# Four projections of two linear-attention layers: fp32 factors split into two rounded parts

## What is computed

```python
xn = layer_norm(x) * norm_w + norm_b
q = xn @ Wq + bq                      # [2, 2048, 512]
k = xn @ Wk + bk + mask               # masked rows far down
v = (xn @ Wv + bv) * mask
q = softmax(q, over one head's columns)
k = softmax(k, over the 2048 rows)
y = q @ (k.T @ v)                     # by head
h = layer_norm(y) * sb_w + sb_b       # then scale and shift by a condition
out = x + silu(h * (1 + scale) + shift) @ Wo + bo
```

## Time and profile before

| | us |
|---|---|
| median of three runs | 5700.12 (5699.62 to 5701.42) |
| profiled execution | 5699.54 |
| its span in the trace | 5697.7 |
| TensorE busy | 5175.6 (91%) |
| VectorE, ScalarE, GpSimd busy | 4163.2, 3142.4, 3289.4 |
| layers 2 and 3, start to end | 4478 to 5088, 5088 to 5698 |

### The profile page before, as it was taken

How to read it: one execution, slowest core, us unless ns; L and a number is a source line. 1 busy time by engine, 2 the same in 40 slices (tenths; PEclk the granted TensorE clock), 3 DMA queues, 4 the chain that set the end, 5 groups by cost and what they waited for, 6 DMA issues and landing times. The chain is left out here.

```text
span 5697.7 us, 58876 instructions
## 1 busy us (share of the span) xinstructions
PE 5175.6 (91%) x18688; PEld 2441.0 (43%) x18688; DVE 4163.2 (73%) x5558; ACT 3142.4 (55%) x5839; POOL 3289.4 (58%) x2200
## 2 busy tenths in 40 slices
PE   7888989888888969989999999999997899989998
PEld 2333333333333324434444444444443455444545
DVE  6999999999999983247777777777763455545454
ACT  4757566665757533327888888888872131312112
POOL 3879797888879761107898898898892000000000
PEclk9999999999999999988999999999998999999999
DMA  4021221212021205321111111111102302021101
GB/s 170 23 104 38 97 88 52 78 49 97 29 104 43 84 11 191 126 82 35 24 35 35 24 35 35 24 35 35 24 13 107 113 26 70 17 106 35 61 26 52
DMA packets 117511, 346.30 MB, mean 61 GB/s; under 512 B 13041, under 2 KB 14289, under 8 KB 102801
## 3 DMA queue, kind: packets, MB, share of 16 engines
q1 hardware_dynamic: 99280, 294.47, 15.8%
q0 software_dynamic: 9216, 33.56, 1.6%
q10 hardware_dynamic: 8704, 14.50, 0.7%
HBM read 274.29 MB, written 67.67 MB: 60 GB/s over the span
## 5 line engine op out<-in xcount | busy, mean ns | idle before, releaser
L425 POOL TENSOR_TENSOR mamba_hc<-mamba_h,mamba_bc 128x1024 f32<-128x1024 f32 x512 | 1218.2, 2379 | 360.7 <-DVE mamba_h L658 307.0
L805 PE MATMUL mamba_y<-mamba_hc,ident 128*128 128x512 f32 x2048 | 997.3, 610 | 272.1 <-POOL mamba_hc L425 269.8
L1282 POOL TENSOR_TENSOR attn_pair_sum<-attn_pair_sum,attn_prob 128x1024 f32<-128x1024 f32 x512 | 1204.2, 2386 | 56.0 <-ACT attn_prob L1397 56.0
L1441 DVE TENSOR_REDUCE attn_mx<-attn_ps_max 128x1 f32<-128x512 f32 x1536 | 966.9, 684 | 318.6 <-PE attn_ps_max L1305 313.7
L1397 ACT ACTIVATE attn_prob<-attn_ps_s 128x512 f32<-128x512 f32 x2048 | 1051.4, 602 | 78.3 <-PE attn_ps_s L1332 78.3
L528 ACT ACTIVATE mamba_da<-mamba_dt,mamba_a_neg 128x512 f32<-128x512 f32 x1024 | 691.1, 689 | 721.6 <-DVE mamba_h L658 718.0
L658 DVE TENSOR_TENSOR_SCAN mamba_h<-mamba_da,mamba_state,mamba_h 128x512 f32<-128x512 f32 x768 | 939.3, 1264 | 1.9 <-ACT mamba_da L528 1.9
L1332 PE MATMUL attn_ps_s<-attn_q_stack,attn_k_stack 100*128 100x512 f32 x2048 | 885.2, 436 | 5.2 <-ACT attn_prob L1397 5.2
L1305 PE MATMUL attn_ps_max<-attn_k_stack,attn_q_stack 98*128 98x512 f32 x2048 | 834.4, 412 | 33.4 <-ACT attn_own_exp L1406 16.6
L805 PEld LDWEIGHTS mamba_y<-mamba_hc,ident 128*128 128x128 f32 x2048 | 366.3, 191 | 856.0 <-POOL mamba_hc L425 458.2
L648 DVE TENSOR_TENSOR mamba_h<-mamba_du,mamba_bc 128x1024 f32<-128x1024 f32 x512 | 618.6, 1208 | 65.2 <-POOL mamba_state L427 56.8
(11 more groups left out here) (240 smaller groups left out, 6545.7 us busy)
## 6 DMA issues: line engine op xcount, KB each, us to landing
mamba_bc<-bc_dram SPq DMA_DIRECT2D x64, 1024.0 KB, 7.2
mamba_w<-in_in_proj_w_T SPq DMA_DIRECT2D x16, 2048.0 KB, 7.7
qk_parts<-qkv_pair POOLq DMA_DIRECT2D x64, 512.0 KB, 3.2
attn_k_stack<-qk_parts SPq DMA_DIRECT2D x96, 256.0 KB
attn_q_stack<-qk_parts SPq DMA_DIRECT2D x96, 256.0 KB
mamba_x_in<-in_x SPq DMA_DIRECT2D x16, 1024.0 KB, 5.5
mamba_w<-in_out_proj_w_T SPq DMA_DIRECT2D x8, 2048.0 KB, 8.4
lin_norm_x<-x_after_L SPq DMA_DIRECT2D x16, 1024.0 KB, 6.0
```

Of the source, the lines that this page charges most:

```text
L425: nc.gpsimd.tensor_tensor(hc[:, gs % HC_SLOTS, :, :], h[:, gs % H_SLOTS, :, :], bc[:, g, G:2 * G, :], ALU.mult).then_inc(s["hc_done"], 1)
L805: mm = nc.tensor.matmul(y[ct % 2][:, :], ident[:, :], hc[:, gs % HC_SLOTS, j, :], start=(g == 0 and j == 0), stop=(g == NG - 1 and j == G ...
L1282: nc.gpsimd.tensor_tensor(pair_sum[(hd * NGRP + g) % 2][:, at], first[:, at], prob[unit % SLOTS][:, at], ALU.add).then_inc(s["sum_done"], 1)
L1441: nc.vector.tensor_reduce(to, ps_max[seq % BANKS][:, :], AX.X, ALU.max, negate=own_block(i)).then_inc(s["bank_read"], 1)
```

## The change

Each factor of the four projections is kept as two tiles of the rounded type: a first part (`xn_first`, `w_first`), the value rounded, and a second part (`xn_second`, `w_second`), the value less its first part, rounded. A product becomes three: first by first, first by second, second by first. The fourth is left out.

- Weights: ScalarE rounds a loaded weight (`cut_w`), GpSimd subtracts (`split_w`). The raw weights land in parts of `v_all` and `k_t` that are free then. Wv and Wo share one pair of tiles, so Wo is loaded and split in each batch and Wv again for the second batch.
- Rows of the projection phase: ScalarE writes the rounded rows as before, VectorE makes the unrounded rows from the same PSUM banks in place of `m1.x` (`full_x`), GpSimd subtracts (`split_x`). The next x is loaded when the subtractions are through.
- Rows of the output phase: ScalarE makes them twice, rounded and unrounded (the second in the place of `m2.x`, which is now `q`), and GpSimd subtracts.
- `m1` and `m2` share the tiles of rounded rows. `x_res` is now `kn`. Banks rotate by chunk (`bank`).
- The k products of the first two blocks and the output products of the first three tiles are ordered so that those with the rows' second part come last.

```diff
+            def load_x(it):
+                sp.wait_ge(s["second_1"], it * KD)
+                norm_load(sp, m1, src, it)
...
+                sp.wait_ge(s["k_turned"], b * QT + 2 * CH // P)
+                load_w(sp, W_VO, 2 * b + 2, "Wo")
...
+            def split_w(i, n):
+                pool.wait_ge(w_cut[i], n)
+                nc.gpsimd.tensor_tensor(w_second[i][:, :, :], w_raw(i, n), w_first[i][:, :, :].bitcast(F32),
+                                        ALU.subtract).then_inc(w_split[i], 1)
+
+            def split_x(m, full, second, it):
+                for k in range(KD):
+                    pool.wait_ge(m.turned, it * KD + k + 1)
+                    pool.wait_ge(s[full], it * KD + k + 1)
+                    nc.gpsimd.tensor_tensor(by_tile(xn_second[:, k, :]), in_x(m, k), by_tile(xn_first[:, k, :].bitcast(F32)),
+                                            ALU.subtract).then_inc(s[second], 1)
...
+                    pe.wait_ge(w_split[W_K], 1)
+                    for mt in range(2):
+                        pe.wait_ge(m1.turned, it * KD + mt + 1)
+                        pe.wait_ge(s["full_1"], it * KD + mt + 1)
+                        k_products(it, mt, ((0, 0), (1, 0)), True, False)
+                    for mt in range(2):
+                        k_products(it, mt, ((0, 1),), False, True).then_inc(s["k_mm"], 1)
+                    for mt in range(2, KD):
+                        pe.wait_ge(s["k_done"], it * KD + mt - 1)
+                        k_products(it, mt, ((0, 0), (1, 0), (0, 1)), True, True).then_inc(s["k_mm"], 1)
...
                             for k in range(KD):
-                                mm = nc.tensor.matmul(mb[used[t % 2]][:, :], m1.xn_t[:, k, t * P:(t + 1) * P], w[which][:, k, :],
-                                                      start=(k == 0), stop=(k == KD - 1))
+                                for i, j in ((0, 0), (0, 1), (1, 0)):
+                                    mm = nc.tensor.matmul(bank(it, 2 + t)[:, :], (xn_second if i else xn_first)[:, k, at],
+                                                          (w_second if j else w_first)[which][:, k, :],
+                                                          start=(k == 0 and i + j == 0), stop=(k == KD - 1 and i == 1))
...
+                    for t in range(TT - 1):
+                        pe.wait_ge(m2.turned, it * KD + t + 1)
+                        pe.wait_ge(s["full_2"], it * KD + t + 1)
+                        o_products(t, ((0, 0), (0, 1)), True, False)
+                    for t in range(TT - 1):
+                        o_products(t, ((1, 0),), False, True).then_inc(s["o_mm"], 1)
+                    pe.wait_ge(s["full_2"], (it + 1) * KD)
+                    o_products(TT - 1, ((0, 0), (0, 1), (1, 0)), True, True).then_inc(s["o_mm"], 1)
...
+            def cut_w(i, n):
+                act.wait_ge(w_in[i], 16 * n)
+                nc.scalar.activation(w_first[i][:, :, :], w_raw(i, n), ACT.Copy).then_inc(w_cut[i], 1)
...
                 def norm(it):
                     act.wait_ge(s["v_mm"], it * TT)
+                    act.wait_ge(s["o_mm"], it // NC_B * NC_B * TT)
...
+                    for k in range(KD):
+                        nc.scalar.activation(in_x(m2, k), by_tile(y_banks(c)[k][:, :]), ACT.Silu, scale=batch_film[:, 0, k:k + 1],
+                                             bias=batch_film[:, 1, k:k + 1]).then_inc(s["full_2"], 1)
...
+                def full_x(it):
+                    dve.wait_ge(s["v_mm"], it * TT)
+                    dve.wait_ge(s["o_mm"], it // NC_B * NC_B * TT)
+                    for k in range(KD):
+                        dve.wait_ge(m1.turned, it * KD + k + 1)
+                        nc.vector.tensor_scalar(in_x(m1, k), by_tile(x_banks(it)[k][:, :]), g[:, k:k + 1], bvec[:, k:k + 1],
+                                                ALU.mult, ALU.add).then_inc(s["full_1"], 1)
```

More of the change, by code:

```diff
@@ L865, with __init__ @@
 class Norm:
-    def __init__(self, r, keep, banks=None):
-        self.x = r.sb("norm_x", [P, TT, D])
-        self.xn_t = r.sb("norm_xn_t", [P, KD, CH])
+    def __init__(self, r, keep, banks=None, x=None, xn=None):
+        self.x = r.sb("norm_x", [P, TT, D]) if x is None else x
+        self.xn_t = r.sb("norm_xn_t", [P, KD, CH]) if xn is None else xn
         self.stats = r.sb("norm_stats", [P, TT, 6])
@@ L888, in norm_load, with norm_dve @@
     sp.dma_start(m.x[:, :, :], rows[bass.ds(it * CH, CH), :].rearrange("(t p) d -> p t d", p=P)).then_inc(m.x_loaded, 16)
-def norm_dve(nc, dve, m, own, it, src):
+def norm_dve(nc, dve, m, own, it, src, read=None):
     for t in range(TT):
@@ L1654, in y_banks, with bank, x_banks, w_raw @@
             return tb if c % 2 else mb
+        def bank(it, i):
+            return mb[(2 * (it % 2) + i) % 4]
+        def x_banks(it):
+            return [bank(it, k) for k in range(KD)] if it else tb
+        def w_raw(i, n):
+            if n == 1:
+                return v_all[:, (i + 1) * KD:(i + 2) * KD, :]
+            return k_t[:, :, D:2 * D] if n % 2 == 0 else k_t[:, :, 2 * D:3 * D]
+        def load_w(engine, i, count, n):
+            engine.dma_start(w_raw(i, count), a[names_of[n]].rearrange("(k p) n -> p k n", p=P)).then_inc(w_in[i], 16)
+        def in_x(m, k):
+            return m.x[:, :, k * P:(k + 1) * P]
+        def by_tile(rows_t):
+            return rows_t.rearrange("p (t j) -> p t j", j=P)
         @block.sync
@@ new lines, in k_products @@
+                def k_products(it, mt, parts, first, last):
+                    for k in range(KD):
+                        cols_of = slice(mt * P, (mt + 1) * P)
+                        for i, j in parts:
+                            if mt == 0:
+                                pe.wait_ge(*((s["second_1"], it * KD + k + 1) if j else (m1.turned, it * KD + k + 1)))
+                            weights = (w_second if i else w_first)[W_K][:, k, cols_of]
+                            rows_t = (xn_second if j else xn_first)[:, k, :]
+                            mm = nc.tensor.matmul(bank(it, mt % 2)[:, :], weights, rows_t, start=first and k == 0 and (i, j) == parts[0],
+                                                  stop=last and k == KD - 1 and (i, j) == parts[-1])
+                    return mm
@@ L1884, in q_bias @@
                         dve.wait_ge(s["q_mm"], it * TT + t + 1)
[L1885 removed]
+                        nc.vector.tensor_tensor(q[:, t, :], bank(it, 2 + t)[:, :], rows[:, 0, :], ALU.add).then_inc(s["q_biased"], 1)
                     dve.wait_ge(s["q_turned"], it * KD)
```

133 lines of the change are left out of this document (84 added, 49 removed).

## The result

The changed kernel takes 5598.40 us (5595.86 to 5599.63) where the kernel before, run beside it, took 5700.77: ratio 0.9819, 95% interval 0.9802 to 0.9836. The forecast was 5588, the range 5545 to 5640. The profiled execution's span is 5594.1; the one of before was 5697.7, so 103.6 us went out of the profile, where the sum said 111.4.

What follows compares the result with a forecast made beforehand. TensorE was taken to bound the kernel. Savings at layer starts, middle chunks, last chunks and output phase sum to 52.8 us in layer 2 and 58.6 in layer 3, together 111.4 from 5699.54: 5588, range 5545 to 5640.

Steps and rivals of the forecast that it cites:

- What bounds: In the two linear layers TensorE is the bound, busy 563 of 610 us in the first.
- The price of a product: Rounded 512-column products in the four projections cost 0.233 us each, 2.55 less per projection and chunk.
- GpSimd's subtraction: Four 128x512 subtractions per chunk and phase at 1.27 us each; upper end 2.54, lower 1.1.
- A middle chunk: Five per layer: 40.0 us instead of 45.58, 27.8 saved per layer, TensorE pausing 1.8 in each.
- cold clock: Rival: the 1.8 pause in every chunk halves TensorE's clock, 45 us, 5633; chance 0.18 together with a partly slower GpSimd.
- The last chunk: Last chunk of a batch: 39.2 us in layer 2, 35.9 in layer 3; 5.4 and 11.2 less per layer.
- The charge for the clock: Layer 2's last chunks: 1.7 us charged for slower transposes after a TensorE pause of about 5.
- The output phase: Output blocks shrink by 2.55, 1.84 or 2.7, one nearly eaten at the batch boundary: 16.6 us less per layer.
- A layer's start: First K waits for Wk in two parts, ending about 0.4 later; q gains 3.43: 3.0 us less per layer.

Runs made afterwards that it cites:

- The undone output projection: Output projection alone put back to full fp32 products, K, q and v left in three rounded products, against the changed kernel: 5633.01 us.
- the fourth product: Second part by second part added in all four projections, 64 instead of 48 products each, against the changed kernel: 5781.09 us.
- the experiment: GpSimd makes each subtraction for the rows twice, one behind the other, against the changed kernel: 5785.92 us.
- The early table: ScalarE makes a one-column exponential behind the rounding of Wv, loading its table before the first chunk's q, against the changed kernel: 5593.05 us.

## Why the prediction was right, and where it was off

**What bounds.** Right: TensorE set the time before, and a cheaper product shortened every part of it. The undone output projection (34.6 against 33.2) and the fourth product (183 against 188) came out as the same sums said.

**The price of a product.** Right: 0.2325, taken from attention's rows as 0.233. The Trainium skill's rule (TensorE: Matmul & The Clock Gate, "Wait — 56ns, not 53.3ns?") would have given 0.2157. At a granted clock of 1.00 the 48 products took 11.15, so it doesn't hold for this type.

**GpSimd's subtraction.** Right: 5.22 for four, 1.3 each, for 1.27 forecast; the rounded type costs GpSimd nothing. This was the term with the widest bounds, and the experiment shows what its upper end would have cost: at twice the time 187 us, more than the whole gain.

**A middle chunk.** 40.2 to 40.5 (once 39.5, in layer 3, where slow first products of K hid its wait) instead of 40.0, by the mechanism that was forecast: the fourth subtraction done 5.1 behind K's start, the third v bias at 13.11 behind q's end (13.09 forecast), the pause 1.6 (1.8). K takes 0.25 longer than the sum said (three times in it the step from one product to the next is 0.08 to 0.1 longer than the rest, and a bank comes late), and the handovers from ScalarE to VectorE to TensorE, which I had put at 0.08 each, take 0.2 more. In ten chunks that makes 2.5. The rival "cold clock" didn't come: in the stretch from 4580.8 to 4593.0 the granted clock is 1.00, behind pauses of 1.6.

**The last chunk.** 39.3 for 39.2 in layer 2, 36.1 for 35.9 in layer 3: the chain through ScalarE and VectorE was read rightly. That the row of the table comes out at 16.6 to the decimal is luck. The charge for the clock, 1.7 a batch in layer 2, was 0.1 in one batch and 2.6 in the other, and layer 2 gained 6.1 for 5.4 where layer 3 gained 10.5 for 11.2.

**The output phase.** The period is 16.5 as forecast, but the gain 30.8 for 33.2. At the batch boundary K waits 2.44 (2.55 forecast). The four batches gained 6.7, 9.1, 8.3 and 6.7 for 7.0, 9.6, 7.0 and 9.6, so the sum was right in its main term and partly lucky in the rest. Most of what is missing lies in layer 3's last block, which gained 0.9 for 2.7. Behind a wait of 2.52 TensorE's eight next products took 3.5 there, at a granted clock of 0.51; behind the same wait in layer 2 the clock stayed at 1.00 (columns as for the busy time above):

```profile
5575.80:5579.30 3.50, 3.46 (x8) 2.80 (x9) 0.00 (x0) 1.79 (x3) 3.50 (x3) 0.51 0.60 207
5024.10:5027.60 3.50, 3.50 (x15) 2.89 (x16) 0.00 (x0) 1.75 (x3) 3.50 (x3) 1.00 0.56 211
```

The third block of each batch gained 1.6 for 1.84. TensorE's speed behind the pause at a phase's start moved the rest, both ways: from the transposes to the first output product layer 3 took 6.7 for 8.2 in its first batch and 7.8 for 6.9 in its second.

**A layer's start.** This step failed: 3.1 measured of 6.0. K began at 4496.24 (4496.6 forecast), ended and gave q's gain as said. But I put what follows q at nothing: ScalarE loads the exponential's table there, 1.28 us, once a layer. It was there before too, and from q's end to the next K the first chunks took 18.0 and 17.8 where the others took 17.2; v's longer products covered the rest. Now it lies on VectorE's row, makes the pause 3.0, and the transposes behind it run at half clock. That stretch then takes 20.2 and 19.4. I had the price of such a pause in hand and applied it to the last chunks only. The early table shows it: with the load out of the way the stretch takes 17.1 and 16.9.

## What to carry to other kernels

When the work of the bound engine shrinks by a fifth, go through the chain of its neighbours' work behind it as it will then stand, one-off work such as table loads included, and look for what becomes late there. Before VectorE work is moved, see what GpSimd does in the time to which it goes: the same instruction was free in one place and cost nearly 2 us a chunk in the other. A term for which TensorE waits in mid-run can cost more than its length: behind waits of 2 to 3 us the clock fell to half in several places here, though not behind each of them.

## What the runs showed that I had not expected

VectorE's multiply and GpSimd's subtraction stretched each other from 2.29 to 3.43 and from 1.28 to 3.31, and fell back when one was moved. Rounded fp32 columns cost about 0.44 ns each by the two widths measured; 0.419 would be a quarter of the full product. Pauses of 1.6 left the clock at 1.00, waits of 1.2, 2.1 and 1.8 with a single product between each left it at 0.50, and of two waits of 2.52 at the same place of the two layers one left it at 1.00 and the other at 0.51.
